# Which engine normalises the tokens, and at which place of its queue

## What is computed

```python
mod = (_silu(L0_c) @ L0_wmod).reshape(B, 6, 1, -1)
sa, ca, ga, sb, cb, gb = (mod[:, n] for n in range(6))
h = _layernorm(x) * (1 + ca) + sa          # (x - mean) / sqrt(var + eps), then scale and shift
q, k, v = h @ query_proj, h @ key_proj, h @ value_proj      # 16 heads, key 16, value 64 wide
attn = softmax(q . k / 4, axis=queries)
x = x + ga * (attn @ v) @ output_proj
h = _layernorm(x) * (1 + cb) + sb
x = x + gb * fp4_ffn(h)                    # gate, up, down with a 4-bit grid
```

## Time and profile before

| | |
|---|---|
| time, 3 runs | median 1822.77 us (1821.62 to 1824.83) |
| the profiled execution | 1823.0 us, its span from first to last instruction 1821.7 us |
| busy | PE 1707.5 us (94%), DVE 1654.8 (91%), ACT 1369.2 (75%), POOL 533.5 (29%) |
| TensorE's mean granted clock | 0.982 |
| preparation of the first sequence | from 0 to about 113 us |
| preparation of the second sequence | from about 727 to about 818 us |

### The profile page before, as it was taken

The page is one execution under the profiler, slowest core; times in us unless marked ns, Lnnn a source line. Parts: engine busy times, 40 slices in busy tenths (PEclk is TensorE's granted clock), DMA queues, the critical chain, the costliest instruction groups (busy, mean ns, idle before and its releaser), DMA issues.

```text
span 1821.7 us, 38065 instructions
## 1 busy us (share of the span) xinstructions
PE 1707.5 (94%) x15122; PEld 820.3 (45%) x15122; DVE 1654.8 (91%) x2343; ACT 1369.2 (75%) x2552; POOL 533.5 (29%) x1007
## 2 busy tenths in 40 slices
PE   6889999999999999799999999999999989999996
PEld 5653222232222322483223222232222488999996
DVE  4589999999999999368999999999999699999995
ACT  3259999999999999338999999999999522232232
POOL 3202222221222222401222122222122436666664
PEclk9899999999999999899999999999999999999998
DMA  5201011110111102220111011110110412222200
GB/s 170 92 12 31 30 32 39 38 42 30 33 38 38 41 31 59 74 80 26 39 38 42 30 33 39 38 41 30 33 39 24 134 61 70 70 70 73 70 12 18
DMA packets 52434, 88.50 MB, mean 49 GB/s; under 512 B 3232, under 2 KB 34848, under 8 KB 52256
## 3 DMA queue, kind: packets, MB, share of 16 engines
q1 hardware_dynamic: 51840, 85.54, 14.4%
q10 hardware_dynamic: 416, 0.53, 0.1%
HBM read 56.69 MB, written 29.36 MB: 47 GB/s over the span
## 4 chain that ended last, share of the span: by engine, by line
PE 51%; ACT 21%; issue 15%; DVE 8%; POOL 4%; POOLq 0%; DVEq 0%; ACTq 0%
PE acc L563 25%; ACT e_sb L753 20%; PE slot L534 8%; PE slot L401 6%; PE acc L401 6%; PE acc L583 4%; POOL e_sb L869 2%; DVE nm L989 1%; PE slot L624 1%; POOL hqT_lo L842 1%; DVE e_sb L1074 1%; DVE e_sb L1075 1%; DVE ost L1000 1%; DVE e_sb L1070 1%; POOL v_sb L1172 0%
## 5 line engine op out<-in xcount | busy, mean ns | idle before, releaser
L989 DVE TENSOR_REDUCE nm<-slot 128x1 f32<-128x1024 f32 x1024 | 1180.9, 1219 | 10.4 <-PE slot L534 10.4
L753 ACT ACTIVATE e_sb<-slot,nm 128x1024 f32<-128x1024 f32 x1024 | 1141.2, 1114 | 26.6 <-DVE nm L989 25.4
L563 PE MATMUL acc<-e_sb,vp 64*64 64x512 f32 x8192 | 1069.5, 596 | 39.1 <-ACT ost L773 38.6
L534 PE MATMUL slot<-stq,stk 64*64 64x512 f16 x4096 | 418.2, 393 | 8.3 <-ACT e_sb L753 8.3
L534 PEld LDWEIGHTS slot<-stq,stk 64*64 64x64 f16 x4096 | 118.5, 104 | 671.7 <-ACT e_sb L753 633.1
L563 PEld LDWEIGHTS acc<-e_sb,vp 64*64 64x64 f32 x8192 | 283.8, 133 | 193.3 <-issue 93.5
L1227 POOL TENSOR_TENSOR dlt<-nm 128x4 f32<-128x4 f32 x128 | 25.4, 199 | 701.8 <-DVE nm L989 701.8
L753 ACT ACTIVATION_READ_ACCUMULATOR e_sb<-slot,nm 128x1 f32 x1024 | 197.3, 193 | 0.0
L1218 POOL TENSOR_TENSOR vp<-v_sb,fac 128x512 f32<-128x512 f32 x128 | 133.4, 1042 | 10.2 <-POOL fac L1208 0.2
L842 POOL TENSOR_TENSOR hqT_lo<-e_sb,hqT_hi 128x640 fp32r<-128x640 f32 x64 | 120.3, 1898 | 50.9 <-ACT hqT_hi L677 50.9
L796 ACT COPY e_sb<-slot 128x256 f32<-128x256 f32 x32 | 11.9, 373 | 159.4 <-PE slot L594 159.4
(11 more groups left out here) (179 smaller groups left out, 1804.9 us busy)
## 6 DMA issues: line engine op xcount, KB each, us to landing
stk<-qk_parts SPq DMA_DIRECT2D x128, 128.0 KB
o_heads<-ost SPq DMA_DIRECT2D x64, 256.0 KB, 3.5
v_sb<-o_heads SPq DMA_DIRECT2D x8, 2048.0 KB, 8.5
v_sb<-in_x SPq DMA_DIRECT2D x16, 512.0 KB, 7.6
qk_parts<-e_sb SPq DMA_DIRECT2D x32, 256.0 KB, 2.2
stq<-qk_parts SPq DMA_DIRECT2D x128, 64.0 KB
out<-e_sb SPq DMA_DIRECT2D x32, 128.0 KB, 1.7
v_sb<-in_wgu SPq DMA_DIRECT2D x1, 1408.0 KB, 14.3
```

What stands on the lines that cost most here:

```text
L534: mm = pe.matmul(slot[s][side * VD:(side + 1) * VD, c * 512:(c + 1) * 512], stk[c * 64:c * 64 + 64, h % 2, i * P + side * VD:i * P + (side ...
L563: mm = pe.matmul(acc[half * VD:(half + 1) * VD, c * 512:(c + 1) * 512], vp[rows, g % 3, gi, half, :], e_v[rows, j % ERING, n0:n0 + 512], s ...
L753: act.activation(e_v[:, j % ERING, half * 1024:(half + 1) * 1024], slot[u % 3][:, :], ACT.Exp, bias=nm[:, g % 4, i, half:half + 1], accum_ ...
L989: dve.tensor_reduce(nm[:, g % 4, i, half:half + 1], slot[u % 3][:, :], AX.X, ALU.max, negate=True).then_inc(maxed.sem)
```

## The change

The six normalisations that GpSimd did are given to VectorE, so that it does all eight. One tally, `xn_made`, counts them in place of two. The waits that held `stats` until a buffer's normalisation had read its mean are gone, as both are now on one engine. The places in VectorE's queue are:

- First sequence: `stats(0, 1)` goes ahead, right behind `normalise(0, 0)` and before the reading of the modulation (`sa`, `a1`, `most`). `normalise(0, 1)` takes its old place, behind `low_tokens(0, 0)` and before `level()`.
- `normalise(b, g + 2)` stands between the second and the third split of group `g` (in group 0 of the first sequence behind `low_tokens(0, 1)`).
- Between the sequences: `stats(1, 0)`, `stats(1, 1)`, `normalise(1, 0)`, `normalise(1, 1)`, where it was `stats`, `normalise` of group 0 and then `stats` of group 1.

GpSimd keeps the inverse roots, and the power of `level()` no longer stands behind a normalisation.

```diff
--- before.py
+++ after.py
@@ -237,7 +237,7 @@
 
         made_ident, made_half, rstd_made, wv_low = tally("made_ident"), tally("made_half"), tally("rstd_made"), tally("wv_low")
         diff_made, tot_made, vp_made = tally("diff_made"), tally("tot_made"), tally("vp_made")
-        wsq_made, root_made, xn_made = tally("wsq_made"), tally("root_made"), tally("xn_made")
+        wsq_made, root_made = tally("wsq_made"), tally("root_made")
         folded, xq_low, hq_low, hid_scaled = tally("folded"), tally("xq_low"), tally("hq_low"), tally("hid_scaled")
         pool_own = own("pool_own")
 
@@ -247,7 +247,7 @@
         wgu_high, wdb_high, xq_high, hq_high = tally("wgu_high"), tally("wdb_high"), tally("xq_high"), tally("hq_high")
         silu_made = tally("silu_made")
 
-        c_silu, mod_cols, xn_first, var_made = tally("c_silu"), tally("mod_cols"), tally("xn_first"), tally("var_made")
+        c_silu, mod_cols, xn_made, var_made = tally("c_silu"), tally("mod_cols"), tally("xn_made"), tally("var_made")
         part_low, wqk_low, tok_low, v_dve = tally("part_low"), tally("wqk_low"), tally("tok_low"), tally("v_dve")
         most_made, ratio_made, even_made = tally("most_made"), tally("ratio_made"), tally("even_made")
         rows_read, rows_made, gu_quant, dn_quant = tally("rows_read"), tally("rows_made"), tally("gu_quant"), tally("dn_quant")
@@ -282,8 +282,7 @@
             return quarter[uses[b][kind, n][0]]
 
         def normalised(b, g):
-
-            return xn_made.past(b * (NG - 1) + g - 1) if g else xn_first.past(b)
+            return xn_made.past(b * NG + g)
 
 
 
@@ -849,8 +848,6 @@
 
         def stats(b, g):
             dve.wait_ge(*got_x[g].past(b))
-            if b or g >= 2:
-                dve.wait_ge(*(normalised(b, g - 2) if g >= 2 else normalised(b - 1, g + 2)))
             for i in range(GROUP):
                 ins = dve.bn_stats(st6[:, g % 2, i, :], x_v[:, g * GROUP + i, :])
             settle(ins)
@@ -859,16 +856,16 @@
             settle(ins)
             dve.tensor_scalar(ve[:, g % 2, :], mv[:, g % 2, :, 1], EPS, None, ALU.add).then_inc(var_made.sem)
 
-        def normalise(eng, b, g):
-            eng.wait_ge(*rstd_made.past(b * NG + g))
+        def normalise(b, g):
+            dve.wait_ge(*rstd_made.past(b * NG + g))
             if b and g < 2:
-                eng.wait_ge(*attended.past(b * JT - 8))
+                dve.wait_ge(*attended.past(b * JT - 8))
             if g >= 2:
-                eng.wait_ge(*tok_turned.past(b * NG + g - 2))
+                dve.wait_ge(*tok_turned.past(b * NG + g - 2))
             for i in range(GROUP):
-                ins = eng.tensor_scalar(xn_r[:, g % 2, i, :], x_v[:, g * GROUP + i, :], mv[:, g % 2, i, 0:1],
+                ins = dve.tensor_scalar(xn_r[:, g % 2, i, :], x_v[:, g * GROUP + i, :], mv[:, g % 2, i, 0:1],
                                         rstd[:, g % 2, i:i + 1], ALU.subtract, ALU.mult)
-            ins.then_inc((xn_made if g else xn_first).sem)
+            ins.then_inc(xn_made.sem)
 
         def low_tokens(b, g):
             dve.wait_ge(*tok_out.past(b * NG + g))
@@ -964,7 +961,7 @@
                 low(dve, wq_lo[:, :, :], wq_s[:, :, :], wq_hi[:, :, :])
                 low(dve, wk_lo[:, :, :], wk_s[:, :, :], wk_hi[:, :, :]).then_inc(wqk_low.sem)
                 low_tokens(0, 0)
-                stats(0, 1)
+                normalise(0, 1)
                 level()
             for g in range(NG):
                 if g + 2 < NG:
@@ -973,6 +970,8 @@
                     part_dve(b, g, r)
                     if b == 0 and g == 0 and r == 1:
                         low_tokens(0, 1)
+                    if g + 2 < NG and r == 1:
+                        normalise(b, g + 2)
                 if g + 2 < NG:
                     low_tokens(b, g + 2)
             for i in range(EARLY):
@@ -1012,8 +1011,9 @@
                     take_values_dve(b, EARLY + j)
                 if j == JT + 2 and b + 1 < B:
                     stats(b + 1, 0)
-                    normalise(dve, b + 1, 0)
                     stats(b + 1, 1)
+                    normalise(b + 1, 0)
+                    normalise(b + 1, 1)
                 if j in (JT + 5, JT + 6) and b + 1 < B:
                     low_tokens(b + 1, j - JT - 5)
                 if j == JT + 2 and b == B - 1:
@@ -1127,7 +1127,8 @@
             settle(dve.tensor_tensor(sc4[:, 1], sc4[:, 0], sc4[:, 3], ALU.mult))
             dve.tensor_copy(scb, sc4[:, 1].unsqueeze(3).to_broadcast([P, 2, B, P])).then_inc(c_silu.sem)
             stats(0, 0)
-            normalise(dve, 0, 0)
+            normalise(0, 0)
+            stats(0, 1)
             dve.wait_ge(*mod_mm.past(0))
             dve.tensor_copy(sa[:, :, :], slot[2][:, 0:4].rearrange("p (k b) -> p k b", b=B))
             dve.tensor_scalar(a1[:, :, :], slot[2][:, 4:8].rearrange("p (k b) -> p k b", b=B),
@@ -1178,12 +1179,10 @@
         def prepare_pool(b):
             if b == 0:
                 inverse_root(0, 1)
-                normalise(pool, 0, 1)
                 pool.wait_ge(*ratio_made.past(0))
                 pool.tensor_tensor(bound[:, 1], bound[:, 0], quarter4[:, :, :], ALU.pow).then_inc(root_made.sem)
             for g in range(2, NG):
                 inverse_root(b, g)
-                normalise(pool, b, g)
             if b == 0:
                 pool.wait_ge(*wv_high.past(0))
                 for k in range(2):
@@ -1229,7 +1228,6 @@
                 if j == JT + 2 and b + 1 < B:
                     inverse_root(b + 1, 0)
                     inverse_root(b + 1, 1)
-                    normalise(pool, b + 1, 1)
                 if j == JT + 2 and b == B - 1:
                     pool.wait_ge(*vp_made.past(B * JG - 1))
                     for n in range(14):
```

## The result

The changed kernel takes 1799.78 us in the median of 4 runs (1796.23 to 1800.94), the kernel before 1822.77. The ratio is 0.9869, with a 95% interval from 0.9852 to 0.9886: 1.3% faster, 23.0 us. The forecast was 1800.0. The profiled execution took 1800.63 us, its span 1799.3, which is 22.4 less than before.

What follows compares the result with a forecast made beforehand. TensorE was taken to idle before transposes, waiting for GpSimd's normalisations, six blocks on the path. 1823.0 profiled less 10.2 (first sequence) and 12.6 (between sequences) gives 1800.2, less 0.2 to the median 1800.0; range 1795.5 to 1806.

Steps and rivals of the forecast that it cites:

- The moves of the transposes: First sequence: transposes of group 2 start at 30.1, not 36.86 (6.8 us gained), of group 3 at 40.7, not 50.95 (10.2).
- the front: First sequence, group 1: stats ahead delays a1 and most by 1.93 us; cost 0.04 us, hidden, up to 0.9 with fast transposes.
- 0.7 lost at group 0: Between the sequences: transposes of group 0 go from 731.63 to 732.3, 0.7 us lost.
- 6.0 gained at the queries: Between the sequences: with no pause before group 1, queries start at 739.9 instead of 745.87, 6.0 us gained.
- 9.2 at group 2: Between the sequences: group 2's transposes come at 746.75, not 755.87, 9.1 us gained.
- 12.6 at group 3: Between the sequences: group 3's transposes come at 756.45, 12.6 us gained, with a cycle of 9.7 where it was 13.2.
- the two halves: The preparations of the first sequence (10.2 us gained) and between the sequences (12.6 us), both subtracted from the profiled time.
- The first gain: First sequence: level()'s power, queued behind GpSimd's normalisation, starts at 20.45 instead of 26.51; ScalarE's first split 6.06 us earlier.
- The rival in which the low clock goes altogether: Transposes and matmuls in both sequences: shorter pauses bring no low clock, some 5 us more saved, 1795; chance 0.08.
- VectorE's longer queue: Both preparations: 24 more VectorE instructions of about 0.34, 8 us more, all where it idled longer than that.
- The rule that spoke against it: Normalisation's engine: by near-equal speeds the cycle would gain next to nothing, time near 1817 by the moved power alone.
- a rival that ends slower: Normalisations on the path: VectorE and GpSimd block one another, about 1827; chance 0.03.

Runs made afterwards that it cites:

- Experiment 2: The kernel before with all of the change in the first sequence only, GpSimd normalising as before in the second; 1812.52 us, ratio 0.9945.
- Experiment 1: The kernel before with only stats(0, 1) moved ahead, behind the first normalisation, GpSimd still doing its six normalisations; 1816.93 us, ratio 0.9967.
- experiment 8: The changed kernel with stats(0, 1) back at its old place behind low_tokens(0, 0); 1801.33 us, ratio 0.9878.
- Experiment 7: As experiment 4, with second-sequence stats and normalisation of groups 2 and 3 also made earlier, and wv_hi rounded one group sooner; 1783.73 us, ratio 0.9779.
- Experiment 3: The changed kernel with each VectorE normalisation block made twice, the same values written again; 1809.41 us, ratio 0.9925.
- experiment 6: The changed kernel with GpSimd also making the first sequence's normalisations of groups 2 and 3, into an unread spare region; 1800.08 us, ratio 0.9869.
- experiment 4: The changed kernel with stats and normalisation of groups 2 and 3 one step further ahead in VectorE's queue; 1788.51 us, ratio 0.9816.
- experiment 5: The changed kernel with normalise(b, g + 2) behind the fourth split of group g instead of the second; 1806.12 us, ratio 0.9899.

## Why the prediction was right

- **The path, term by term.** The moves of the transposes were forecast at 6.8 and 10.2 us in the first sequence and came at 6.7 and 10.4, or 6.4 and 10.1 without the 0.3 us by which the whole execution began earlier. What is missing at group 2 was lost at the front, which the prediction had at nothing on the path: TensorE waited 0.66 us for `most`, the queries of group 0 kept the low clock's length longer, and group 1 turned 11.5 us behind the first transposes where the forecast had 11.2. Between the sequences, counted from the start of `stats(1, 0)`, which moved from 727.04 to 717.21, that is by 9.8: 0.7 lost at group 0, forecast 0.7; 6.0 gained at the queries, forecast 6.0; 9.2 at group 2, forecast 9.1; 12.6 at group 3, forecast 12.6. Experiment 2 showed that the two halves add.
- **The first gain was more than TensorE's wait.** That the power of `level()` had queued behind GpSimd's normalisation was read from two rows. Experiment 1 moved it from 26.51 to 21.52 by the early step alone, with GpSimd's block still in front of it, and experiment 8 to 23.35 by the exchange alone; both together gave 20.25.
- **The clock.** The rival in which the low clock goes altogether did not come. After idle times of 2.65, 2.13 and 3.12 us some matmuls still took the low clock's length (transposes in 1.70, 1.84 and 1.37 us); after none or 1.05 us they took 1.09 or 1.03. A part of it came: behind group 3 of the second sequence the low clock cost 0.7 us less than before (13.65 us from its transposes to the values, for 14.35; the granted clock of the first 5 us of it was 0.66, where it was 0.51), so that half gained 13.3 us and not 12.6. In the first sequence it went the other way: from group 3 to the values it was 16.48 us for 16.18, with the low clock's matmuls 0.7 us longer there. Experiment 7 removed the pauses, and in both of its stretches the granted clock is 1.00.
- **VectorE's longer queue** cost what was said: 8.4 us more busy time (1663.2 for 1654.8), and on the path only the blocks, at 1.38 each. Experiment 3 showed that these are exposed one for one, but for the groups 1. The bill was small because a block is 1.38 us and not 4.83; only at the groups 1 did something hide it.
- **The rule that spoke against it** ("GPSIMD Engine Reference" of the Trainium skill, "Engine selection": one-input work is "roughly line-rate" on GpSimd) does not hold here: 1.22 us against 0.41 in the earlier trace rows. Experiment 3, where one more VectorE block cost 1.4 us on the path, and the earlier trace rows, where a GpSimd block had cost 5.54, bear out the rows.
- **What was luck.** That the median fell 0.2 us from the forecast says little, as the four runs lie between 1796.2 and 1800.9. In the profiled execution errors of the terms cancel: 9.8 us up to `stats(1, 0)` for 10.2 forecast, 13.3 from there to the second values for 12.6. The first output projection moved by 23.2 (from 1443.79 to 1420.58), and the feed-forward part behind it took 0.8 us longer, so the span fell by 22.4.
- **What no run separates.** Between the sequences the change does two things, it exchanges the engine and it puts `stats(1, 1)` before `normalise(1, 0)`. Their shares are read from the rows of one trace; no experiment has one without the other.
- **The lock** ("SBUF — State Buffer" of the Trainium skill, "Who interferes with whom", by which the second of the two waits for the whole instruction of the first when VectorE is in its two-port form) was left as a rival that ends slower, and no run here tests it. The prediction took the normalisation for VectorE's fast form. Rows of the kernel before speak against that: at the same size a one-input instruction with constants takes 0.29 us, and the normalisation, whose mean and root are columns with one value for each token, takes 0.41, as long as instructions that read two tensors or PSUM. So experiment 6 shows only what this pair of instructions does to one another, 0.08 us at most on a single one of VectorE's. Had VectorE waited for one whole GpSimd instruction, 1.2 us would show. These are the rows, VectorE in time in the kernel before, an input out of PSUM, one tensor and PSUM, and one tensor with constants:

```profile
82.00 0.41 DVE L923 TENSOR_SCALAR v_sb<-slot 128x256 f32<-128x256 f32 x1
82.45 0.42 DVE L924 SCALAR_TENSOR_TENSOR v_sb<-v_sb,slot 128x256 f32<-128x256 f32 x1
82.90 0.29 DVE L926 TENSOR_SCALAR v_sb<-v_sb 128x256 f32<-128x256 f32 x1
```

## What to carry to other kernels

When an engine idles before a short step again and again, follow the chain of waits round one whole cycle, and price an edit by which steps it takes out of that cycle: here the same early step was worth 6 us or 1 to 2, by what else was in it. Moving work to a faster engine that is also fuller pays when it idles at just those places, and its place in that engine's queue counted too: two splits later cost 6 us, a step ahead gave 11 more. Before moving an instruction ahead, look at what the receiving queue waits for next: in experiment 4, where two such steps went ahead, it cost at most the 1.3 us for which the queries then waited.

## What the runs showed of the hardware

- On VectorE a one-input `tensor_scalar` of 128 x 256 float32 out of SBUF took 0.29 us with constants and 0.41 us with two operands that hold one value for each partition.
- GpSimd's four normalisations slowed from 4.83 to 5.5 or 5.6 us beside one two-input subtraction (`hT_lo`) of 128 x 1024 on VectorE, but only to 5.06 beside four one-input instructions of VectorE of 0.41 us.
- Behind like transposes of group 3 in the first sequence the matmuls kept the low clock's length for 2.6 us in the kernel before, 3.3 in the changed one and 5.2 in experiment 1, counted from the start of the transposes. So the place of the first values can differ by a microsecond or so between executions.
- The last part of the kernel, which no experiment touches, is not of one length. From the first output projection to the end it took 377.9 us in the profiled execution before, 378.7 after, 377.6 in experiment 3, 381.2 in experiment 4 and 384.5 in experiment 5. A difference of a few microseconds between two single executions can come from there alone; distances within a stage are the better witness: from `stats(1, 0)` to the second sequence's values it was 43.07, 43.03 and 43.03 us in the three kernels that are alike there (the changed one, experiments 6 and 8).
